# Cross attention in 32-row score products: four query layouts instead of sixteen

## The reference, cut to what matters

```python
q = _split_heads(query @ Wq.T + bq, B, T)      # query = layernorm(x)
k = _split_heads(key @ Wk.T + bk, B, T)        # key = value = ctx
v = _split_heads(value @ Wv.T + bv, B, T)
scores = einsum('bhqd,bhkd->bhqk', q, k) / sqrt(8)
weights = softmax(scores, axis=-1)
x = x + tanh(g) * (merge_heads(einsum('bhqk,bhkd->bhqd', weights, v)) @ Wo.T + bo)
```

## Time and profile before

| | |
|---|---|
| profiled execution | 2175.77 us, of which the span is 2173.8 us |
| cross attention (start to L929) | 0 to 359.9 us |
| rest of the kernel | 359.9 to 2173.8 us |
| busy over the span | PE 92%, DVE 74%, ACT 50%, POOL 41% |
| residual add L652, one per sequence | 8 times, 76.6 to 359.4 us |
| a combined iteration, L652 to L652 | 41.2 us (159.69 to 200.91) |
| PE busy from 159.7 to 200.9 us | nearly all but some 5 us, most of these at its end |

### The profile page before, as it was taken

The page is one execution under the profiler, slowest core; times in us unless marked ns, Lnnn a source line. Parts: engine busy times, 40 slices in busy tenths (PEclk is TensorE's granted clock), DMA queues, the critical chain, the costliest instruction groups (busy, mean ns, idle before and its releaser), DMA issues.

```text
span 2173.8 us, 84521 instructions
## 1 busy us (share of the span) xinstructions
PE 1993.4 (92%) x35280; PEld 1294.1 (60%) x35280; DVE 1612.6 (74%) x3316; ACT 1092.6 (50%) x1911; POOL 891.2 (41%) x1166
## 2 busy tenths in 40 slices
PE   6988987789999999999999999999999999999995
PEld 2333332456666666666766666767676766666763
DVE  5565563667878788787878787878787878787872
ACT  2333333345555555555555555656565646464643
POOL 1000000444545555455545454545454646463540
PEclk9999999899999999999999999999999999999996
DMA  1000100455556555556555565555655556554550
GB/s 61 5 5 10 53 0 1 69 85 82 84 82 123 93 84 84 83 111 104 86 80 89 97 108 90 89 79 96 114 96 87 84 84 112 103 86 81 84 83 21
DMA packets 73218, 166.72 MB, mean 77 GB/s; under 512 B 16592, under 2 KB 23504, under 8 KB 72272
## 3 DMA queue, kind: packets, MB, share of 16 engines
q0 software_dynamic: 36864, 100.71, 34.0%
q1 hardware_dynamic: 36320, 65.55, 11.8%
HBM read 20.45 MB, written 1.05 MB: 10 GB/s over the span
## 4 chain that ended last, share of the span: by engine, by line
PE 54%; DVE 18%; DMA 14%; issue 9%; POOL 4%; ACT 1%; POOLq 0%; DVEq 0%; SPq 0%; ACTq 0%
DMA big<-big 13%; PE ps L948 12%; PE ps L983 8%; PE ps L871 6%; PE ps L959 5%; PE ps L1020 4%; DVE big L770 4%; DVE big L767 3%; PE ps L1037 3%; POOL big L452 3%; PE ps L1007 3%; PE ps L892 2%; DVE big L801 2%; PE ps L876 2%; DVE big L788 2%
## 5 line engine op out<-in xcount | busy, mean ns | idle before, releaser
L452 POOL DMA_DIRECT2D big<-big x768 | 607.5, 1494 | 66.8 <-DVE big L770 56.1
L948 PE MATMUL ps<-big,wn_sb 128*128 128x256 f32 x1536 | 394.4, 393 | 25.5 <-issue 15.0
L520 ACT ACTIVATE big<-ps 128x512 f32<-128x512 f32 x384 | 229.1, 597 | 331.8 <-PE ps L948 325.4
L948 PEld LDWEIGHTS ps<-big,wn_sb 128*128 128x128 f32 x1536 | 273.2, 190 | 103.6 <-issue 46.5
L778 DVE TENSOR_TENSOR big<-big,ps 128x512 f32<-128x512 f32 x384 | 243.2, 682 | 103.3 <-DMA big<-big 52.4
L533 ACT ACTIVATE big<-ps 128x512 f32<-128x512 f32 x192 | 114.7, 598 | 371.3 <-PE ps L983 371.3
L783 DVE TENSOR_REDUCE top<-ps 128x8 f32<-128x512 f32 x192 | 123.3, 684 | 202.8 <-PE ps L1007 202.8
L767 DVE TENSOR_TENSOR big<-ps,tab 128x512 f32<-128x512 f32 x384 | 257.9, 682 | 9.3 <-ACT big L520 9.3
L770 DVE TENSOR_TENSOR big<-ps,tab 128x512 f32<-128x512 f32 x384 | 257.6, 681 | 0.0
L443 POOL TENSOR_TENSOR big<-big 128x512 f32<-128x512 f32 x96 | 121.9, 1270 | 294.2 <-ACT big L537 294.2
L1091 PE MATMUL ps<-big,wo_sb 128*128 128x256 f32 x768 | 213.1, 380 | 2.2 <-issue 2.2
(11 more groups left out here) (146 smaller groups left out, 3219.1 us busy)
## 6 DMA issues: line engine op xcount, KB each, us to landing
big<-big POOLq DMA_DIRECT2D x768, 128.0 KB, 4.9
big<-big SPq DMA_DIRECT2D x96, 256.0 KB, 3.9
big<-big SPq DMA_DIRECT2D x96, 192.0 KB, 4.0
wn_sb<-in_wn SPq DMA_DIRECT2D x6, 1024.0 KB, 9.1
wn_sb<-in_wn SPq DMA_DIRECT2D x6, 512.0 KB, 4.7
wo_sb<-in_wo SPq DMA_DIRECT2D x6, 512.0 KB, 3.4
w_sb<-in_w SPq DMA_DIRECT2D x6, 341.0 KB, 2.9
w_sb<-in_w SPq DMA_DIRECT2D x6, 192.0 KB, 2.9
```

What stands on the lines that cost most here:

```text
L452: eng.dma_start(rot[to:to + 32, at:at + 4, :], src[32 * r:32 * r + 32], accum_op=ALU.add).then_inc(added[i], 16)
L520: eng.activation(sq[:, two, :], ps[:, i % 2, :].rearrange("p (a t) -> p a t", a=2), ACT.Square).then_inc(sq_d, 1)
L948: mm = eng.matmul(ps[:, k % 2, a * T:a * T + T], wn_sb[:, u * P:u * P + P], sT, start=True, stop=True)
```

## The change

`score(n)` becomes `scores(s)`, s = 0 to 7, for the two heads 2s and 2s+1 (in the kernel's order of heads, `hd`, in which head i lies in the 32 partitions from 32 * (i % 4), as number i // 4 of four). A product takes only these 32 rows of `kT` and of the queries, 256 columns wide: for each key half one product for head 2s and one for head 2s+1, in different groups of 32 rows and into different banks. Then one `onehot` product of 32 rows and 512 columns for each of the two heads. A bank holds one head with both key halves, instead of two heads with one key half.

`row_scores` likewise reads 32 rows: the two products of one n use the same group of rows and the same bank, those of n+1 the next group and the other bank.

Since the other 96 rows aren't read, one masked layout serves four heads. `hmask` has 4 columns, and `qpadb` and `qpad` have 4 layouts instead of 16; DVE makes the 4 of `qpadb`, ACT the 4 of `qpad` after its exponentials, and L631 is gone from DVE. `mcol` is widened to 128 columns (with a memset at the start), so that the transposes bring each maximum to its own group of rows; `mrow` and `onehot` have 128 rows. The constant `c_onehot` is 256 KB instead of 128 KB.

On ACT `exps` counts heads instead of pairs, and the order of its work stays. The order on PE is written anew (at the end of the diff), and each `scores(s)` and each row product n begins with an increment of a new semaphore `x_go` that nobody waits for; in the code of later stages L994 is such an increment.

```diff
-    onehot = np.zeros((H, H, P), f)
-    onehot[np.arange(H), np.arange(H), :] = 1
-    hmask = np.zeros((P, H), f)
-    hmask[p, p // XD] = 1
+    onehot = np.zeros((P, 4, P), f)
+    onehot[p[m < 4], m[m < 4], :] = 1
+    hmask = np.zeros((P, 4), f)
+    hmask[p, m // XD] = 1
...
-        qpad = view(H * T, H, T)
-        qpadb = view(H * T // 2, H, T, dt=BF16)
+        qpad = view(4 * T, 4, T)
+        qpadb = view(4 * T // 2, 4, T, dt=BF16)
...
-        mcol = sb("mcol", [P, NT, H])
-        mrow = sb("mrow", [H, T], BF16)
+        mcol = sb("mcol", [P, NT, P])
+        mrow = sb("mrow", [P, T], BF16)
...
-                    for i in range(H // 2, H):
-                        eng.activation(qpad[:, i, :], qT, ACT.Copy, scale=hmask[:, hd[i]:hd[i] + 1]).then_inc(xpad2, 1)
+                    for j in range(4):
+                        eng.activation(qpad[:, j, :], qT, ACT.Copy, scale=hmask[:, j:j + 1]).then_inc(xpad, 1)
...
-                    for i in range(H):
-                        eng.tensor_scalar(qpadb[:, i, :], qT, hmask[:, hd[i]:hd[i] + 1], None, ALU.mult).then_inc(xpadb, 1)
+                    for j in range(4):
+                        eng.tensor_scalar(qpadb[:, j, :], qT, hmask[:, j:j + 1], None, ALU.mult).then_inc(xpadb, 1)
...
-                    if X2:
-                        eng.wait_ge(xsc, b * H)
-                    for i in range(H // 2):
-                        eng.tensor_scalar(qpad[:, i, :], qT, hmask[:, hd[i]:hd[i] + 1], None, ALU.mult).then_inc(xpad, 1)
...
+                        eng.sem_inc(x_go, 1)
+                        rows = slice(32 * (pr % 4), 32 * (pr % 4) + 32)
                         for a in range(2):
-                            mm = eng.matmul(ps[:, n % 2, a * T:a * T + T], qpadb[:, 2 * pr + a, t_ * P:t_ * P + P], kTb,
-                                            start=True, stop=True)
+                            mm = eng.matmul(ps[:, n % 2, a * T:a * T + T], qpadb[rows, 2 * (pr // 4) + a, t_ * P:t_ * P + P], kTb[rows, :],
+                                            start=True, stop=True, skip_group_check=True)
...
+                def scores(s):
+                    if s == 0:
+                        eng.wait_ge(cast, CASTS)
+                        eng.wait_ge(xkt, b)
+                        eng.wait_ge(xpad, b * 4)
+                        eng.wait_ge(xmr, b + FREE)
+                    if s >= 2:
+                        eng.wait_ge(xex, b * H + (2 * s - 2 - H))
+                    eng.sem_inc(x_go, 1)
+                    two = (2 * s, 2 * s + 1)
+                    for kt in range(NT):
+                        for i in two:
+                            rows = slice(32 * (i % 4), 32 * (i % 4) + 32)
+                            eng.matmul(ps[:, 2 + i % 4, kt * T:kt * T + T], kT[rows, kt * P:kt * P + P], qpad[rows, i // 4, :],
+                                       start=kt == 0, stop=False, skip_group_check=True)
+                    for i in two:
+                        rows = slice(32 * (i % 4), 32 * (i % 4) + 32)
+                        eng.matmul(ps[:, 2 + i % 4, :].rearrange("p (a t) -> p a t", a=2), onehot[rows, i // 4, :],
+                                   mrow[rows, :].rearrange("p (a t) -> p a t", a=1).to_broadcast((32, NT, T)),
+                                   start=False, stop=True, skip_group_check=True).then_inc(xsc, 1)
...
+                if X1:
+                    tokens()
+                if X2:
+                    scores(0)
+                    scores(1)
+                if X1:
+                    normed_tokens()
+                if X2:
+                    weigh(0)
+                    scores(2)
+                if X1:
+                    projections()
+                if X2:
+                    scores(3)
+                    weigh(1)
+                for n, s in ((0, None), (2, 4), (4, 5), (6, "w"), (8, 6), (12, 7)):
+                    if X2 and s == "w":
+                        weigh(2)
+                    elif X2 and s:
+                        scores(s)
                     if X1:
-                        if pr == 0:
...
+                        row_scores(n, n + (4 if n in (8, 12) else 2))
                 if X2:
                     weigh(3)
```

More of the change, by code:

```diff
@@ L397, in _ @@
             eng.memset(vpad, 0.0).then_inc(zero, 1)
+            eng.memset(mcol[:, :, :], 0.0).then_inc(zero, 1)
             eng.memset(xs[:, :, 0:1], 0.0).then_inc(zero, 1)
@@ L460, in _, with exps @@
             eng.preload_act_table_set("natural_log_exp_and_others")
-            eng.wait_ge(zero, 3)
+            eng.wait_ge(zero, 4)
             def cross_body(b, X1, X2):
-                def exps(pr):
-                    for n in (2 * pr, 2 * pr + 1):
+                def exps(first, last):
+                    for n in range(first, last):
                         eng.wait_ge(xsc, b * H + (n + 1 - H))
@@ L498, in cross_body @@
                     eng.wait_ge(xmt, b + 1)
-                    eng.activation(mrow[:, 0:T], ps[0:H, 0, 0:T], ACT.Copy).then_inc(xmr, 1)
+                    eng.activation(mrow[:, 0:T], ps[:, 0, 0:T], ACT.Copy).then_inc(xmr, 1)
             cross(eng, cross_body)
@@ L891, in weigh @@
                                 w = vpad[:, kt, h, :] if bank == 6 else xones[:, h % 4, :]
-                                mm = eng.matmul(ps[32 * g:32 * g + 32, bank, 0:T], w, xP[:, (2 * (i // 2) + kt) % 8, i % 2, :],
+                                mm = eng.matmul(ps[32 * g:32 * g + 32, bank, 0:T], w, xP[:, i % 8, kt, :],
                                                 start=q == 0 and kt == 0, stop=q == 3 and kt == 1, skip_group_check=True)
                     mm.then_inc(xav, 1)
-                for pr in range(PAIRS):
-                    if X1:
-                        if pr == 0:
-                            tokens()
-                        elif pr == 1:
-                            normed_tokens()
-                        elif pr == 2:
-                            projections()
-                    for half in range(2):
-                        if X1 and pr >= 3:
-                            row_scores(*((0, 1), (1, 2), (2, 3), (3, 5), (5, 6), (6, 8), (8, 10), (10, 12), (12, 13), (13, 14))
-                                       [2 * (pr - 3) + half])
-                        if X2:
-                            score(2 * pr + half)
-                    if X2 and pr in (2, 4, 6):
-                        weigh(pr // 2 - 1)
-                if X1:
-                    row_scores(14, 16)
+                if X1:
+                    tokens()
+                if X2:
+                    scores(0)
+                    scores(1)
+                if X1:
+                    normed_tokens()
+                if X2:
+                    weigh(0)
+                    scores(2)
+                if X1:
+                    projections()
+                if X2:
+                    scores(3)
[5 more added lines that the diff above has]
+                        scores(s)
+                    if X1:
+                        row_scores(n, n + (4 if n in (8, 12) else 2))
                 if X2:
```

82 lines of the change are left out of this document (33 added, 49 removed).

## The result

The changed kernel takes 2149.16 us, the median of four runs (2146.73 to 2152.02), beside 2188.53 us for the kernel before on the same chip (four runs, 2184.47 to 2193.87). The ratio is 0.9828, with an interval of 0.9806 to 0.985: faster by 1.7%, within the range, 19 us above the forecast of 2130. The profiled execution takes 2149.13 us. Against the 2175.77 us of the profiled one before, that is 26.6 us less, where the sum said 57.6.

What follows compares the result with a forecast made beforehand. PE's own instruction stream was taken as the bound, then the idle end. Savings of 51.8 + 3.2 + 6.9 less 4.3 gave 57.6 us: 2175.8 to 2118.2, plus 11.1, rounded to 2130 us; range 2108 to 2164.

Steps and rivals of the forecast that it cites:

- the main case: Whole kernel: the time comes out as the terms sum, 2108 to 2150 us; chance 0.68.
- Score products: PE in combined iterations: paired calls of 1.08 us, eight in 8.6 us instead of 20.5; 11.0 us saved after shape changes.
- the rival of no overlap: Score calls: the two heads' products don't run at once, all 8.6 us come back, about 2190 us, no change; chance 0.06.
- New waits: PE in each combined iteration: `weigh(1)` 1.4 us, `weigh(2)` 1.0, row products 2.2, together 4.6 us lost.
- The rival of evacuation: DVE and ACT emptying PSUM: waits half as large again or more, 2 to 3 us per iteration, 2145 to 2155; chance 0.08.
- The 1.0 us ahead of L838 stays, as the chain over the normed tokens isn't changed.: PE's wait for the normed tokens in a combined iteration: stays at 1.0 us, nothing added to the sum.
- The clock "is left as it is": PE's granted clock: half speed for about 3.4 us after each idle end, 1.7 us lost per iteration, unchanged in the sum.
- Clock low for one to three more stretches: PE clock in combined iterations: one to three more low stretches per iteration, 2142 to 2166 us; chance 0.06.
- L631: End of each combined iteration on DVE: without these copies the reciprocal starts 1.0 us earlier.
- Semaphores: `x_go` increments, 24 per iteration at 51 ns: half exposed, 4.3 us lost in seven iterations.
- First and closing half: Half iterations at both ends: 3.2 us saved by fewer copies in the first, net 6.9 us in the closing one.
- the carried term: Whole kernel: runs' median lies 11.1 us above the profiled execution, added to 2118.2 us to give 2129.3.

Runs made afterwards that it cites:

- The kernel with the same rows: Against "Layer norm first on ACT": both heads of a score call read the same 32 rows, the first head's; ratio 1.0314 to the kernel before.
- Layer norm first on ACT: Against the changed kernel: ACT does the layer norm's logarithm and exponential ahead of exponentials 0 and 1 again; 2123.12 us, ratio 0.9748; second time 2128.98 us.
- the kernel with one head after the other: Against the changed kernel: in each score call both products of one head come first, then both of the other; ratio 0.9848 to the kernel before.
- eight copies put back: Against "Layer norm first on ACT": eight unread DVE copies of 128 x 256 stand between the last maximum and the reciprocal; ratio 0.9721 to the kernel before.
- a repetition: The changed kernel run again without any edit; 2144.34 us, ratio 0.9824 to the kernel before.
- The reordered kernel: Against the changed kernel: next layer norm moved mid-iteration, previous residual into the next iteration, other PE work ahead of each `weigh`; 2068.34 us, ratio 0.949.

## Why the prediction was right and where it failed

**The time and the mechanism.** The time is within the range, the mechanism only in part. The change is 39.4 us (2188.53 to 2149.16) where 57 were forecast. Two of the prediction's own signs came out against it: L652 to L652 is 38.6 us and not near 33.8, and the clock is at 0.5 in the middle of iterations. That 2149.16 lies 0.8 us inside the main case (2108 to 2150) is luck.

**Bound.** Right that PE's stream bound the kernel and that its scores were half of it.

**Score products.** Right. Four products of 256 columns in pairs cost 0.86 us between row products and 0.97 among 128-row work; the whole call is 1.03 us there and 1.28 here, with its changes of shape, against 1.08 and 0.1 to 0.2 for the changes in the sum. The kernel with the same rows shows the alternative: 1.83 us (200.58 to 202.41) and a ratio of 1.031. The weight on L998 over L1007 was right, and the rival of no overlap would have been worse than "no change", since its waits and its clock came on top. The Trainium skill (TensorEngine Tiling (Array Packing), Key Properties) says that tiles in different places of the array can work at the same time; the call of 1.13 us beside 1.99 agrees, in fp32.

**New waits.** Right in size: `weigh(1)` 1.17 us (1.4 in the sum), `weigh(2)` 1.01 (1.0), the row products 1.9 (2.2). The rival of evacuation isn't needed.

**The step that failed: "The 1.0 us ahead of L838 stays, as the chain over the normed tokens isn't changed."** It did change. The text ahead of the prediction says that the order of ACT's work stays, and this is wrong. In the kernel before, the layer norm's two activations stood ahead of the first exponential; in the changed one `exps(0, 2)` stands ahead of them, and its two exponentials can't start before the first score call is done. ("Layer norm first on ACT" turns this back.) The wait became 2.17 us, and PE's clock fell behind it, so that `weigh(0)` took 3.5 us instead of 1.9, and the last score call and row products took 1.0 us more, also at half clock. With the order undone `weigh(0)` waits 0.4 us instead, so these make 3.5 of the 3.7 us between 34.2 and 37.9. Undoing this order alone gave 34.2 us and 24 to 27 of the 31 us back. `weigh(3)` at half clock, 1.2 us more than in the sum, is in both kernels; waits of 4.1 us instead of 4.6 offset part of it, and the rest wasn't traced.

**The clock "is left as it is".** Mis-sized. The sum took one short stretch of 1.2 GHz per iteration, as before; there were some 17 us instead of 4. "Clock low for one to three more stretches" stood at 0.06 with 2142 to 2166, and this is where the time came out. Its price was too high: the sum took 1.7 us for a low stretch of 3.4. Iterations of 37.9, 39.6 and 41.0 us, the last in the kernel with one head after the other, go with clocks of 0.82, 0.76 and 0.67. That is some 14, 19 and 27 us at half clock, and roughly 0.2 to 0.35 us of time for each such microsecond. So the share of the low clock alone isn't its price, and order and clock can't be added up. The reading that PE held the clock at 66 to 100% busy leaves out a stretch of the kernel before with 1.91 of 3.4 us busy (111.7 to 115.1), which held it too.

**L631.** 1.0 us per iteration in the sum; the idle end did shrink from 3.38 to 2.37 us, as said. But `weigh(3)` now begins only behind the last row products and takes 3.1 us, and with eight copies put back the reciprocal starts as it does without them. The term is worth nothing here.

**Semaphores.** 4.3 us in the sum. Where the clock is equal, half of the increments' time is exposed, as the sum took (0.2 us for eight); in the whole it can't be told from a repetition.

**First and closing half.** Ahead of the first residual add 8.1 us came, of 10.1 with the semaphores. In the closing half 1.2 came of 6.4:

```profile
303.83 1.93 PE L897 MATMUL ps<-big 128*32 128x256 f32 x16 [1.64 <-ACT big L471]
```

The first `weigh` waits 1.64 us for ACT, the other three 1.85 each, 7.2 in all (6.4 in the sum), and each runs at half clock for a good part (1.3 to 1.96 us for a half instead of 1.07). The stage's granted clock is 0.70 where it was 0.99. The kernel with eight copies back shows what this costs: from one `weigh` to the next it takes 5.36 us at full clock (280.47 to 285.83), 7.0 at half. So most of the shortfall is the low clock.

**Profile and median.** The 11.1 us carried from the profiled execution to the median stand beside the first profile of the kernel before only; for the changed one the profiled execution (2149.13) is the median. By the profile the sum was 31 us too low, by the median 19; the carried term hid 11 of them.

**A slip without effect.** The stage from 118.1 to 325.5 us holds five combined iterations, not six (5 x 41.4 = 207 us); nothing was added up from it.

## What to carry to other kernels

When a stage is made shorter, walk the order of every engine again, and above all what stands ahead of a short chain on an engine that seemed to have room: here two exponentials of 0.6 us ahead of a layer norm cost nearly 4 us per iteration. A saved microsecond of TensorE is worth its full price only while TensorE stays busy; here waits opened, the mean clock fell from 0.95 to 0.78 with them, and part of the gain went back. So plan the work that fills the waits together with the change. Compare stretches at equal clock before calling a cost nothing. The reordered kernel got three times the gain of the change (5.1% against 1.7) out of the same products.

## What the runs showed of the hardware

- Products of 32 rows in two groups and two banks overlap almost fully in fp32 (1.13 against 1.99 us for the same eight records), and it doesn't matter whether they are issued in turns or two by two (0.97 and 0.96 us for the four products).
- The clock fell to 1.2 GHz not only behind idle waits but behind a stretch with 32-row row products in which PE was busy 2.54 of 3.4 us; with row products of 128 rows it held at 2.56 of 3.4. `weigh(3)` behind it shows this in every iteration of both. But the reordered kernel, with 32-row row products spread in twos, held 1.00 over iterations of 26.4 us, so the rows alone don't decide, and this is a lead and no rule.
- A semaphore increment of 51 ns ahead of such products is half exposed: 0.2 us for eight of them in a stretch at full clock (6.15 against 6.37 us).
- Which iterations have long stretches at 1.2 GHz differs between kernels that differ in nothing costly (calls in another order, 0.71 against 0.76). The cause is open.
